# The band's mask in the shifted layers: laid into the scores' PSUM bank by a ScalarE copy, instead of an opening matrix product

## The reference, cut to what matters

```python
for i in range(DEPTH):                       # DEPTH = 6
    x = attn_layer(shift_tokens(x), Wqkv[i], q_scale[i], k_scale[i], Wo[i]) + x
    x = ffn_layer(shift_tokens(x), ln_g[i], ln_b[i], W1[i], b1[i], W2[i], b2[i]) + x
# in attn_layer, 16 heads of 64, windows of 32 tokens; a window sees itself and the one before
mask = (it < jb) | (it > jb + w) | (jb == -1)
sim = jnp.einsum('bhwie,bhwje->bhwij', bq, bk2) * QK_SCALE
sim = jnp.where(mask, -jnp.finfo(sim.dtype).max, sim)
attn = jax.nn.softmax(sim, -1)
out = jnp.einsum('bhwij,bhwje->bhwie', attn, bv2)
```

## Time and profile before

| | us |
|---|---|
| median of 3 runs (5028.64 to 5030.45) | 5028.88 |
| the profiled execution's own time | 5030.85 |
| its span, first to last instruction | 5029.1 |
| PE busy | 4220.7 (84%) |
| DVE busy | 3670.4 (73%) |
| ACT busy | 2816.3 (56%) |
| POOL busy | 2236.8 (44%) |

### The profile page before, as it was taken

One profiled execution on the slowest core, in us unless ns is written; L12 is line 12 of the kernel. 1 busy time (PEld: TensorE's weight loads), 2 busy tenths in 40 slices (PEclk: granted clock), 3 DMA queues, 4 the chain that ended last, 5 costly groups with the idle time before them and its releaser, 6 DMA issues. The chain is left out here.

```text
span 5029.1 us, 113839 instructions
## 1 busy us (share of the span) xinstructions
PE 4220.7 (84%) x40234; PEld 2422.8 (48%) x40619; DVE 3670.4 (73%) x8812; ACT 2816.3 (56%) x5023; POOL 2236.8 (44%) x1403
## 2 busy tenths in 40 slices
PE   8969999999999999999999999999999546456426
PEld 5635555545555555555554555555555325244314
DVE  7878878878888888888887887888887453554440
ACT  3436666666666666666666666666666455342001
POOL 0026555555555555555555555555555001300025
PEclk9989999999999999999999999999999668685558
DMA  1023222322232222322223222232222000000202
GB/s 38 1 67 68 53 59 56 75 60 58 54 77 58 60 56 57 77 56 58 59 54 76 62 55 58 55 76 59 58 54 54 16 11 1 5 0 9 68 6 29
DMA packets 186665, 245.77 MB, mean 49 GB/s; under 512 B 88549, under 2 KB 129255, under 8 KB 186088
## 3 DMA queue, kind: packets, MB, share of 16 engines
q1 hardware_dynamic: 180904, 239.95, 20.5%
q0 software_dynamic: 5632, 4.33, 0.7%
HBM read 41.13 MB, written 14.30 MB: 11 GB/s over the span
## 5 line engine op out<-in xcount | busy, mean ns | idle before, releaser
L1229 POOL TENSOR_TENSOR f_rot_a<-f_rot_a,f_norm 128x1024 f32<-128x1024 f32 x384 | 730.9, 1903 | 1107.1 <-DVE f_norm L1072 1074.6
L1221 POOL TENSOR_TENSOR f_rot_a<-f_rot_a,f_rot_b 128x1024 f32<-128x1024 f32 x384 | 907.5, 2363 | 353.7 <-issue 298.3
L830 PE MATMUL f_bank<-f_w_vo,f_xs_t 128*64 128x512 f32 x3072 | 828.4, 617 | 9.6 <-ACT f_vo L1297 9.6
L1297 ACT ACTIVATE f_vo<-f_bank 128x512 f32<-128x512 f32 x768 | 457.6, 596 | 579.0 <-PE f_bank L830 572.7
L1288 ACT ACTIVATE f_squares<-f_bank 128x512 f32<-128x512 f32 x768 | 459.2, 598 | 330.1 <-PE f_bank L817 244.5
L1051 DVE TENSOR_TENSOR f_rot_a<-f_bank,f_rot 128x512 f32<-128x512 f32 x768 | 527.6, 687 | 85.9 <-POOL f_rot_a L1221 41.7
L1054 DVE TENSOR_TENSOR f_rot_b<-f_bank,f_rot 128x512 f32<-128x512 f32 x768 | 515.1, 671 | 0.0
L863 PE MATMUL f_bank<-f_k_t,f_q_t 128*32 128x128 f32 x12288 | 415.1, 276 | 77.5 <-issue 47.7
L1058 DVE TENSOR_REDUCE f_sums<-f_squares 128x16 f32<-128x1024 f32 x384 | 465.4, 1212 | 3.1
L1100 DVE TENSOR_REDUCE f_stat<-f_score 128x8 f32<-128x512 f32 x384 | 262.1, 682 | 280.2 <-ACT f_score L1314 280.2
L1309 ACT ACTIVATE f_k_t<-f_bank 64x512 f32<-64x512 f32 x768 | 450.5, 587 | 4.8 <-PE f_bank L852 0.3
(11 more groups left out here) (445 smaller groups left out, 7251.6 us busy)
## 6 DMA issues: line engine op xcount, KB each, us to landing
f_vo_off<-f_vo SPq DMA_DIRECT2D x1152, 128.0 KB, 2.3
f_vo_off<-f_vo SPq DMA_DIRECT2D x384, 64.0 KB, 2.0
f_w_qk<-in_Wqk SPq DMA_DIRECT2D x12, 512.0 KB, 5.4
f_vo_dram<-f_vo_pair SPq DMA_DIRECT2D x48, 128.0 KB, 1.8
f_x_shifted<-s_all SPq DMA_DIRECT2D x48, 128.0 KB
f_x_shifted<-s_all SPq DMA_DIRECT2D x48, 127.0 KB
f_w_vo<-f_vo_dram SPq DMA_DIRECT2D x10, 512.0 KB, 3.9
e_w<-in_e_W SPq DMA_DIRECT2D x2, 2048.0 KB
```

The source lines that it names most:

```text
L830: done = nc.tensor.matmul(bank[V][64 * n:64 * n + 64, :], x, w_vo[:, 4 * g:4 * g + 4, n, :], start=True, stop=True)
L1221: nc.gpsimd.tensor_tensor(rot_a[:, slot, :, :], rot_a[:, slot, :, :], rot_b[:, g, :, :], ALU.add).then_inc(rot_summed, 1)
L1229: nc.gpsimd.tensor_tensor(heads, heads, over(norm[:, 16 * g:16 * g + 16], [128, 16, HEAD_DIM]), ALU.mult).then_inc(qk_normed, 1)
L1297: nc.scalar.activation(vo[:, g, 2 * (t % 2) + j, :], flat(V), ACT.Copy).then_inc((va_copied, vb_copied)[j], 1)
```

## The change

A semaphore `seeded` is added. Ahead of the loop PE opens bank S once with identity times band. In the loop no opening product is left: per chunk ACT copies the band's 128x512 from SBUF into bank S, right behind its copy of k, once DVE is through with the bank, and the score products (start=False, as before) add onto it. PE waits for `seeded` in place of `shifted`.

```diff
         scores_done, shifted, exped, inverted = sem("scores_done"), sem("shifted"), sem("exped"), sem("inverted")
+        s_opened, seeded = sem("s_opened"), sem("seeded")
...
             pe.wait_ge(zeroed, 2)
+            nc.tensor.matmul(flat(S), ident_bf[:, :], band[:, 0, :], start=True, stop=True).then_inc(s_opened, 1)
...
             def scores(p, t, g):
                 pe.wait_ge(k_t_made, count(p, 2 * t + g))
 
-                pe.wait_ge(shifted, count(p, 2 * t + g - 1))
-                nc.tensor.matmul(flat(S), ident_bf[:, :], band[:, t % 2, :], start=True, stop=True)
+                pe.wait_ge(seeded, count(p, 2 * t + g))
...
             act.wait_ge(zeroed, 2)
+            act.wait_ge(s_opened, 1)
...
-            for semaphore in (scores_done, q_turned, k_turned, q_done, k_done, va_done, vb_done, prob_turned, mixed):
+            for semaphore in (seeded, scores_done, q_turned, k_turned, q_done, k_done, va_done, vb_done, prob_turned, mixed):
                 act.sem_inc(semaphore, AHEAD)
...
+            def seed(p, t, g):
+
+                act.wait_ge(shifted, count(p, 2 * t + g - 1))
+                nc.scalar.activation(flat(S), band[:, t % 2, :], ACT.Copy).then_inc(seeded, 1)
...
                     if on(r - 1):
                         copy_k(p, r - 1, 0)
+                        seed(p, r - 1, 0)
                         copy_values(p, r - 1, 1, 1)
...
                     if on(r - 1):
                         exponential(p, r - 1, 0)
                         copy_k(p, r - 1, 1)
+                        seed(p, r - 1, 1)
```

## The result

The changed kernel takes 4962.78 us (median of 4 runs, 4960.14 to 4965.32) against 5028.76 (4 runs, 5027.20 to 5030.45) of the kernel before: a ratio of 0.9874, 95% interval 0.9862 to 0.9886, so 66 us less. The forecast was 4961.0.

The account below looks back on a forecast made before the run. PE's queue was taken to set the pace, except at fixed waits. Of 2.25 us of openings a pass, 1.42 us were kept; times 48 that is 68 us, so 5029 - 68 = 4961 us, range 4915 to 5030.

Parts of the forecast that it names:

- Price of an opening: PE, start to start: 0.32 us at g=1; at g=0 0.22 us, but 0.31 in r=1; 2.25 us a pass.
- the rows after L817 speak against 0.22 us: PE in r=1, g=0: after the projection of k the opening costs 0.31 us, not the 0.22 of the skill's rule.
- 0.22 us each: Case: every opening on PE is worth 0.22 us, 1.12 us a pass, 54 us in all, 4975 us; chance 0.17.
- The seed: ACT's copy of the band into the bank, per chunk: 0.60 us of duration and 0.50 us of queue.
- r=1, the wait for the store: At g=0 the 0.31 us opening is lost and 0.20 us added, through square of k, DVE's rotation and store.
- r=2 and r=3, the table loads: ACT's chain of gelus and table loads starts before r=2's g=1 opening; its 0.32 us goes into PE's L852 wait.
- The sum: Kept per pass: 0.22 + 0.32, -0.20 + 0.32, 0.22 + 0, 0.22 + 0.32: 1.42 us; times 48, 68 us.
- No wait for a seed: PE's scores start no later: r=1 level, r=0 0.5 us to spare, r=2 and r=3 about 0.8, g=1 free.
- All kept: Case: the waits at L909 and L852 move along, so 48 x 2.25 = 108 us is saved, 4921 us; chance 0.15.
- Nothing moves: Case: another loop (DVE or ACT) is as long as PE's, so 5029 us, within 10; chance 0.08.
- slower: Case: the seed's 0.5 us ahead of the square of k reaches PE in four rounds; 50 us more, 5079; chance 0.14.

Follow-up runs that it names:

- experiment 1: Mask left out of the kernel before: neither opening product nor ACT copy, the first score products start the bank; 4951.8 us.
- experiment 8: The kernel before with the opening product issued twice in a row in each chunk; 5103.4 us.
- experiment 3: The changed kernel with seeds only in r=1 at g=0 and r=2 at g=1, opening products in all other chunks; 5033.4 us.
- experiment 2: The kernel before plus one ACT copy of the band per chunk into an unused SBUF tile, where the seed would stand; 5041.4 us.
- experiments 5 and 6: DVE's store of the feed-forward result moved ahead of the rotation of k (g=1): in the changed kernel 4916.7 us, in the kernel before 5000.8 us.
- experiment 7: The changed kernel with a spare ACT copy of the band to SBUF right ahead of each seed; 5035.9 us.

## Why the forecast was right, step by step

- **Price of an opening.** At g=1 0.32 to 0.33 and at g=0 0.21 to 0.22 us, as read from pairs of equal neighbours. The exception is r=1, 0.31 in the forecast and 0.21 measured. The pair was no twin: what followed the projection of k in the row without opening was another product of the full array (L938), and the step to the score products costs 1.06 us by itself, not 0.96 (experiment 1). So the forecast's remark that the rows after L817 speak against 0.22 us was wrong. It changed nothing in the sum, since that opening was counted as lost. The case "0.22 us each" falls by the first product's own price (1.33 to 1.01), though its number is what a second product costs (experiment 8).
- **The seed.** 0.583 us for 0.60. In the queue it costs 1.70 - 1.21 = 0.49 us from the k copies to the values' copy; 0.50 had been taken.
- **r=1, the wait for the store.** Forecast: the opening's 0.31 lost and 0.20 more, a wait of 0.9. Measured: 0.22 lost, 0.15 more (experiment 3; 0.13 by experiment 1 against the changed kernel), a wait of 0.77. The chain is the one named: seed, square of k, rotation of k, store; experiment 2 lengthens it by a copy alone, experiments 5 and 6 take it away. The 0.20 was mis-sized by 0.05 to 0.07. In ACT's queue the square of k stands 2.19 us behind the k copies' start (2371.21 to 2373.40) where it stood 2.01 behind (2560.69 to 2562.70 in the earlier trace rows): 0.18 us later, as the 0.49 of the seed first fills the gaps that ACT had there.
- **r=2 and r=3, the table loads.** Forecast: the 0.32 us of r=2 g=1 handed back in full, because the chain of table loads starts ahead of it. Measured: 0.32 handed back, so the term is right. But it came back earlier in the round than I had put it: at the values' product (L832, 0.19 to 0.52), which waits for a copy of the values that ACT makes behind the three gelus. The wait at L854 stayed 1.15, where the forecast had it grow to about 1.5. That the chain starts ahead of the opening is read from the trace; experiment 3 shows that the 0.32 us is handed back there, but no run took the gelus or the table load away.
- **The sum.** 1.42 us a pass forecast, 1.47 measured; the 0.05 is the seed in r=1. 68 us forecast, 66 measured, since I multiplied by 48 where 44 passes are steady and the three that fill the pipeline gave 2 us together. Two errors of opposite sign, 48 x 0.05 = 2.4 us one way and some 4 the other: that the time was met within 2 us is in part luck. The 73.6 us a pass of the forecast was of the same kind, a mean with the filling passes in it; a steady pass is 74.43.
- **No wait for a seed.** Right for the steady passes of the changed kernel; outside them the first chunk of all waited 1.37 us for its seed. The reason given for g=1, that the mixing and the values' products stand between, was wrong for r=0: those products cover the k copy, but only with about 0.2 us to spare (experiment 7). Had the seed been one copy longer, the forecast would have failed there: for a seed of 1.2 us it had a loss of 34 us, and the kernel with the spare copy lost 73.
- **The other cases.** "All kept" needs both waits to move with the rest; experiments 5 and 6 show that removing one of them is worth 0.35 us a pass to the change, so in the kernel as it is they don't move. "Nothing moves" and "slower" are refuted by the time. The slower one's premise, that what stands ahead of the square of k reaches PE in all four rounds, is contradicted by experiment 2: there a copy of 0.64 us did so in one round only.

## What to carry over

Taking an instruction off the engine that sets the pace brings its start-to-start price only where no wait follows whose cause began ahead of it; list those waits first, and read the price between the same neighbours with and without it, since the same product was worth 0.22 or 0.32 us by what stood around it. Then look behind the wait that takes the gain back: here it was an unrelated store queued behind late work on DVE, and moving that store up brought 46 us more, where the whole change had brought 66. When such waits are cleared one by one, the next one stands closer each time (0.98, then 0.26 us a pass), and the room that the new work has left is worth measuring by a spare copy before more is put into that queue.

## What the runs showed that I had not expected

- **ACT into PSUM and into SBUF.** The tile f_spare in the kernel with the late seed, to set beside the 583 ns of the seed:

```profile
L1318 ACT ACTIVATE f_spare<-f_band x384: 629/630/633, 350.9 to 3899.4; 128x512 f32<-128x512 bf16 x192
```

  The same 128x512 out of the same bf16 table takes 47 ns longer into SBUF. The Trainium skill (ScalarE: Activation LUTs, "Step-by-step: what each stage is for") says that ScalarE is faster toward PSUM than toward SBUF; both runs agree with it.
- **DVE standing behind POOL.** In r=1 of the changed kernel DVE normalises four pieces of 128x128 (L1131) while POOL scales q and k (L1230) and then weighs the probabilities (L1236). DVE's timeline, then POOL's:

```profile
2368.16 1.79 DVE L1131 TENSOR_SCALAR f_f_n<-f_x_shifted,f_f_mv,f_norm 128x128 f32<-128x128 f32 x1
...
2369.87 1.08 DVE L1131 TENSOR_SCALAR f_f_n<-f_x_shifted,f_f_mv,f_norm 128x128 f32<-128x128 f32 x1
```

```profile
2367.97 1.90 POOL L1230 TENSOR_TENSOR f_rot_a<-f_rot_a,f_norm 128x1024 f32<-128x1024 f32 x1 [0.17 <-POOL f_rot_a L1222]
2369.83 1.04 POOL L1236 TENSOR_TENSOR f_prob<-f_score,f_stat 128x512 f32<-128x512 f32 x1
```

  The last two take 0.59 us together; the first takes 1.79 and the second 1.08. The first ends at 2369.95, POOL's L1230 at 2369.87; the second ends at 2370.95, POOL's L1236 at 2370.87. All four take 3.30 us here and 2.98 in the kernel before, where the first two end 0.08 us behind POOL's instructions, too. The Trainium skill (GPSIMD Engine Reference, "1. Specifications") says that GpSimd shares its SBUF interfaces with VectorE and contends with DVE instructions in a 2-port mode or with two SBUF inputs, which would explain it if these run in such a mode. No run took POOL's instruction away, so this is argued, not shown. It matters here: DVE's part of r=1 before the rotation came only 0.3 us earlier in the pass, where PE came 0.54 earlier. DVE's sum ended at 2373.98 (2372.78 + 1.20), ACT's square of k at 2373.99, so DVE was just short of setting the pace itself, and without the seed it does (experiment 1).
- **PE's clock.** In the kernel with the late exponential PE stood still 1.96 us in every pass, and in about every second one the granted clock then was 0.50 (the 1.2 GHz level) for some 3.4 us, which made that pass 1.64 us longer (74.25 against 72.61); waits of 1.15 us at L854 never did that in any of the other kernels, whose granted clock is 1.00 in every steady pass.
